# A graph and attention layer on one core: the query products bank by bank in place of four banks together, and early loads for them into the dead x area

## The reference

```python
xn = _layernorm(x)
x = x + gnn(xn, edges) + mix(xn)        # two RGAT convolutions; linear attention
x = x + ffn(_layernorm(x))              # int8 product

# mix, 12 heads of 64
q, k, v = split(xn @ W_qkv + b_qkv)
qf, kf = _phi(q), _phi(k)
kv = einsum('bhnd,bhne->bhde', kf, v)
y = einsum('bhnd,bhde->bhne', qf, kv) / max(einsum('bhnd,bhd->bhn', qf, kf.sum(2)), EPS)
mix = y @ W_out + b_out

# one RGAT convolution (4 heads, then 1)
xr = einsum('nd,rdf->rnf', x, W);  oi, oj = xr[etype, dst], xr[etype, src]
alpha = leaky_relu(oi @ q + oj @ k, 0.2)
a = softmax of alpha over the edges of each dst
out = segment_sum(a * oj, dst) + b
```

## Time and profile before

| | us |
|---|---|
| median of 3 runs (lowest, highest) | 1672.69 (1670.72, 1677.49) |
| the profiled execution | 1673.72 |
| its span | 1672.0 |
| TensorE busy | 1574.0 (94%) |
| VectorE busy | 1313.5 (79%) |
| ScalarE busy | 809.4 (48%) |
| GpSimd busy | 144.4 (9%) |
| mean granted TensorE clock | 0.978 of full |

### The profile page before, as it was taken

The page is one execution under the profiler, slowest core; times in us unless marked ns, Lnnn a source line. Parts: engine busy times, 40 slices in busy tenths (PEclk is TensorE's granted clock), DMA queues, the critical chain, the costliest instruction groups (busy, mean ns, idle before and its releaser), DMA issues.

```text
span 1672.0 us, 34410 instructions
## 1 busy us (share of the span) xinstructions
PE 1574.0 (94%) x10567; PEld 1139.5 (68%) x10568; DVE 1313.5 (79%) x2633; ACT 809.4 (48%) x1074; POOL 144.4 (9%) x280
## 2 busy tenths in 40 slices
PE   5899998988999999999999999989999999999987
PEld 4566675666556666699999999976555555555544
DVE  7699968989489999288898998972774577777795
ACT  6331115552235664378888888962222233333352
POOL 3000000000100000000000000000000143333340
PEclk9999998999999999999999999989999999999998
DMA  6111115520456663540132033023766521101212
GB/s 208 37 60 59 60 48 175 165 81 29 133 190 217 201 199 115 177 131 31 62 94 62 31 115 118 14 89 98 210 204 187 203 79 56 53 3 56 89 38 93
DMA packets 129294, 178.54 MB, mean 107 GB/s; under 512 B 15509, under 2 KB 100606, under 8 KB 129202
## 3 DMA queue, kind: packets, MB, share of 16 engines
q1 hardware_dynamic: 129202, 177.38, 33.7%
HBM read 120.47 MB, written 56.88 MB: 106 GB/s over the span
## 4 chain that ended last, share of the span: by engine, by line
PE 71%; issue 15%; DVE 7%; ACT 2%; DMA 2%; DVEq 1%; POOL 0%; SPq 0%; POOLq 0%; ACTq 0%
PE ps L2219 23%; PE ps L2173 14%; PE ps L2279 7%; PE ps L2278 7%; PE ps L1993 4%; PE ps L2084 3%; PE ps L1980 2%; PE ps L1981 2%; PE ps L1982 2%; DVE oh_q L1472 1%; PE ps L2290 1%; PE ps L2156 1%; DVE oh_p L1473 1%; PE ps L2036 1%; ACT q_m L1092 1%
## 5 line engine op out<-in xcount | busy, mean ns | idle before, releaser
L2219 PE MATMUL ps<-xrh,pf 128*128 (+1 forms) x2400 | 399.0, 329 | 4.8 <-DVE pf L1758 4.8
L2219 PEld LDWEIGHTS ps<-xrh,pf 128*128 128x128 f32 x2400 | 392.5, 190 | 11.2 <-issue 9.0
L1980 PE MATMUL ps<-w_hi,xt_hi 128*128 128x384 f16 x600 | 197.6, 329 | 10.0 <-DVE ev_t L1507 3.4
L2278 PE MATMUL ps<-x,ph 128*128 (+1 forms) x600 | 195.2, 325 | 11.8 <-POOL pl L991 11.8
L1758 DVE SCALAR_TENSOR_TENSOR pf<-vb,CT 128x1260 f32<-128x1260 f32 x118 | 172.8, 1468 | 33.6 <-PE ps L2219 33.6
L1981 PE MATMUL ps<-w_lo,xt_hi 128*128 128x384 f16 x600 | 197.4, 329 | 0.0
L1982 PE MATMUL ps<-w_hi,xt_lo 128*128 128x384 f16 x600 | 197.2, 329 | 0.0
L2279 PE MATMUL ps<-x,ph 128*128 (+1 forms) x600 | 196.5, 328 | 0.0
L1472 DVE TENSOR_SCALAR oh_q<-pat,codeT,neg_w 125x630 f16<-125x630 uint16 x420 | 185.0, 441 | 13.8 <-PE ps L1993 7.7
L1754 DVE SCALAR_TENSOR_TENSOR vb<-vb,tb 128x1260 f32<-128x1260 f32 x118 | 170.0, 1466 | 12.7 <-ACT vb L1226 11.8
L1666 DVE CUSTOM_DVE_ANT_0 tt_junk<-kbc,mb 126x1260 bf16<-126x1260 f32 x120 | 169.1, 1466 | 11.7 <-issue 11.7
(11 more groups left out here) (266 smaller groups left out, 2359.1 us busy)
## 6 DMA issues: line engine op xcount, KB each, us to landing
qbc<-tq_d SPq DMA_DIRECT2D x12, 1260.0 KB, 6.5
wst<-in_L_gnn_W SPq DMA_DIRECT2D x60, 192.0 KB, 3.2
xr_d<-ev SPq DMA_DIRECT2D x60, 192.0 KB, 2.0
x_d<-ev SPq DMA_DIRECT2D x60, 192.0 KB, 2.4
mb_d<-mb SPq DMA_DIRECT2D x30, 310.1 KB
mb<-mb_d SPq DMA_DIRECT2D x30, 310.1 KB
xrh<-xr_d SPq DMA_DIRECT2D x3, 2880.0 KB, 15.5
x<-x_d SPq DMA_DIRECT2D x2, 3840.0 KB, 18.1
```

The lines of the kernel that those rows point to most:

```text
L1980: pe.matmul(ps[:, bank, 0:CW], a_hi, hi[:, k, :], start=(k == 0), stop=False)
L2219: mm = pe.matmul(out[b], pf[j][:, b * DB:b * DB + P], x, start=(first and b % 2 == 0), stop=False, skip_group_check=True)
L2278: pe.matmul(ps[:, bank, 0:CW], p, cols(off, off + CW), start=start, stop=False, skip_group_check=True)
```

## The change

The loops of the query products are turned: bank outermost, then the six chunks, then the three split steps. Each bank's 18 matmuls follow each other, and its `q_done` is signalled when they are done. Counted in steps of three matmuls (m from 0 to 23 in a block), windows stand at 8, 16 and the end, weight tiles at every fourth. ScalarE's and VectorE's work in a block is put in an order to match: exponentials and outputs of banks 0 and 1 after the second window's one-hots, those of 2 and 3 later, one weight tile of the next block between them. Tile 0 is drawn ahead of the first block.

The loads of q, k, the three biases and weight tiles 0 to 3 move on SyncE from behind `kvs_done` to between the key windows' and the value windows' stores, into the area of x; tiles 4 and 5 stay behind `kvs_done`. Since the first weight buffer now covers `orow`, its load moves behind all windows' stores.

```diff
--- before.py
+++ after.py
@@ -166,17 +166,17 @@
-        wt = [place(f"wt{j}", [P, D], F32, (148480 if j < 3 else 76864) + 3072 * j) for j in range(6)]
+        wt = [place(f"wt{j}", [P, D], F32, (67584, 86080, 89152, 92224, 148480, 151552)[j]) for j in range(6)]
...
-        qk = place("qk", [P, K6, 2, 2 * H], F16, 158016)
-        qk2 = place("qk2", [P, K6, 2, 2], F16, 158272)
+        qk = place("qk", [P, K6, 2, 2 * H], F16, 95552)
+        qk2 = place("qk2", [P, K6, 2, 2], F16, 95744)
...
-        qkn = place("qkn", [P, K6, 2, H], F32, 157696)
-        qkn2 = place("qkn2", [P, K6, 2], F32, 157888)
+        qkn = place("qkn", [P, K6, 2, H], F32, 95296)
+        qkn2 = place("qkn2", [P, K6, 2], F32, 95488)
...
@@ -620,6 +620,26 @@
+            def wq_load(t):
+
...
+            sp.wait_ge(ln_done, NB)
+            sp.dma_start(qkn[:, :, 0, :], q1.rearrange("(k p) h -> p k h", p=P), allow_slow_non_contiguous=True).then_inc(qk_ready, 16)
...
+            for t in range(4):
+                wq_load(t)
             for c in range(2):
@@ -631,25 +651,7 @@
                 store_window(sp, W_S + k, cb, k % 2)
 
             sp.wait_ge(kvs_done, 2)
-            sp.dma_start(qkn[:, :, 0, :], q1.rearrange("(k p) h -> p k h", p=P), allow_slow_non_contiguous=True).then_inc(qk_ready, 16)
...
-            for t in range(6):
+            for t in range(4, 6):
                 wq_load(t)
             sp.wait_ge(ob_step, 6)
             sp.dma_start(ob_d.rearrange("j (p c) -> p j c", c=K6), osplit[:, :, :]).then_inc(ob_io, 16)
@@ -658,15 +660,15 @@
                     for t in ((0, 1), (2, 3), (4,), (5,))[u] if QW == 4 else ((0, 1), (2, 3), (4, 5))[u]:
                         wq_load(6 * q + t + 6)
                     store_window(sp, W_Q + QW * q + u, cc_, (QW * q + u) % 2)
-                if q == 0:
-                    sp.wait_ge(ob_io, 16)
-                    sp.dma_start(orow[:, :], ob_d[:, :]).then_inc(ob_io, 16)
                 if q == 1:
                     chunk_load(7)
             for i in range(NB):
                 for w in block_windows(i):
                     store_window(sp, w, cc_, (w - W_Q) % 2)
 
+            sp.wait_ge(wt_lo_done, WT_TILES)
+            sp.wait_ge(ob_io, 16)
+            sp.dma_start(orow[:, :], ob_d[:, :]).then_inc(ob_io, 16)
             sp.wait_ge(y_lo, 2 * NB)
             sp.wait_ge(wt_used, WT_TILES)
             sp.wait_ge(ct_out[0], 16 * 31 + 16)
@@ -1075,23 +1077,35 @@
                     act.wait_ge(wt_used, t - 2)
                 act.activation(wt_hi[t % 3][:, :], wt[t % 6][:, :], ACT.Copy, scale=SPLIT).then_inc(wt_hi_done, 1)
 
+            def exponential(q, g):
+
+                n = q * NRG + g
+                act.wait_ge(q_done, n + 1)
+                if n >= NRG:
+                    act.wait_ge(q_out, n - NRG + 1)
+                act.activation(q_m[g][:, :], ps[:, g, 0:RG], ACT.Relu, bias=nbq[:, q:q + 1], scale=-1.0).then_inc(q_mm, 1)
+                act.wait_ge(q_mm, n + 1)
+                act.activation(q_m[g][:, :], q_m[g][:, :], ACT.Exp, scale=-1.0).then_inc(q_ee, 1)
+
             act.wait_ge(bq_done, 1)
+            wt_high(0)
             for c in range(2):
                 for fb in range(3):
                     q = 3 * c + fb
                     wa = W_Q + QW * q
-                    for k in range(K6):
-                        if k in (2, 4, 5)[:QW - 1]:
-                            late_out(wa + (2, 4, 5).index(k))
-                        wt_high(6 * q + k)
-                    for g in range(NRG):
-                        n = q * NRG + g
-                        act.wait_ge(q_done, n + 1)
-                        if n >= NRG:
-                            act.wait_ge(q_out, n - NRG + 1)
-                        act.activation(q_m[g][:, :], ps[:, g, 0:RG], ACT.Relu, bias=nbq[:, q:q + 1], scale=-1.0).then_inc(q_mm, 1)
-                        act.wait_ge(q_mm, n + 1)
-                        act.activation(q_m[g][:, :], q_m[g][:, :], ACT.Exp, scale=-1.0).then_inc(q_ee, 1)
+                    wt_high(6 * q + 1)
+                    late_out(wa)
+                    wt_high(6 * q + 2)
+                    wt_high(6 * q + 3)
+                    exponential(q, 0)
+                    exponential(q, 1)
+                    wt_high(6 * q + 4)
+                    late_out(wa + 1)
+                    wt_high(6 * q + 5)
+                    exponential(q, 2)
+                    if q + 1 < K6:
+                        wt_high(6 * q + 6)
+                    exponential(q, 3)
                     late_out(wa + QW - 1)
                 w_hi_part(C_O + c)
 
@@ -1571,28 +1585,41 @@
                 dve.wait_ge(wt_hi_done, t + 1)
                 dve.scalar_tensor_tensor(wt_lo[k % 3][:, :], wt[k][:, :], SPLIT, wt_hi[k % 3][:, :], ALU.mult, ALU.subtract).then_inc(wt_lo_done, 1)
 
-            def query_block(q):
+            def query_out(q, g):
+
+                n = q * NRG + g
+                dve.wait_ge(q_ee, n + 1)
+                dve.scalar_tensor_tensor(sub(QF, q)[:, g * RG:(g + 1) * RG], ps[:, g, 0:RG], sub(bq1, q), q_m[g][:, :],
+                                         ALU.add, ALU.max).then_inc(q_out, 1)
+
+            def query_block(q, more=True):
 
                 wa = W_Q + QW * q
-                for k in range(K6):
-                    wt_low(6 * q + k, k)
-                    if k in (1, 3, 4)[:QW - 1]:
-                        count_part(wa + (1, 3, 4).index(k) + 1)
-                for g in range(NRG):
-                    n = q * NRG + g
-                    dve.wait_ge(q_ee, n + 1)
-                    dve.scalar_tensor_tensor(sub(QF, q)[:, g * RG:(g + 1) * RG], ps[:, g, 0:RG], sub(bq1, q), q_m[g][:, :],
-                                             ALU.add, ALU.max).then_inc(q_out, 1)
+                wt_low(6 * q + 1, 1)
+                count_part(wa + 1)
+                wt_low(6 * q + 2, 2)
+                wt_low(6 * q + 3, 3)
+                query_out(q, 0)
+                query_out(q, 1)
+                count_part(wa + 2)
+                wt_low(6 * q + 4, 4)
+                wt_low(6 * q + 5, 5)
+                query_out(q, 2)
+                if more:
+                    wt_low(6 * q + 6, 0)
+                query_out(q, 3)
                 count_part(wa + QW)
 
+            wt_low(0, 0)
             count_part(W_Q)
             dve.wait_ge(ct_out[0], 16 * (3 * NB // 2 + 2) + 16)
             dve.wait_ge(ct_out[1], 16 * (3 * NB // 2 + 1) + 16)
             dve.wait_ge(bq_done, 1)
             query_block(0)
             w_lo_part(5)
-            with dve.Fori(1, K6) as q:
+            with dve.Fori(1, K6 - 1) as q:
                 query_block(q)
+            query_block(K6 - 1, False)
 
             def normalised(i):
 
@@ -2065,26 +2092,27 @@
                 for fb in range(3):
                     wa = W_Q + QW * (3 * c + fb)
                     of_w = [window(pe, wa + u)[1:] for u in range(QW)]
-                    for k in range(K6):
-                        if k in (2, 4, 5)[:QW - 1]:
-                            u = (2, 4, 5).index(k)
-                            count_window(wa + u, 6, *of_w[u])
-                        t = 6 * (3 * c + fb) + k - 2
-                        if t == 0:
-                            pe.wait_ge(kvd_done, 2)
-                            pe.wait_ge(qk_ready, 70)
-                        if t >= 0:
-                            wq_tile(t)
-                        w_h, w_l = w_hi[cc % 2][:, k, fb * P:(fb + 1) * P], w_lo[cc % 2][:, k, fb * P:(fb + 1) * P]
-                        for step, (w, t) in enumerate(((w_h, xt_hi), (w_h, xt_lo), (w_l, xt_hi))):
-                            for g in range(NRG):
-                                n = (3 * c + fb) * NRG + g
-                                if k == 0 and step == 0 and n >= NRG:
-                                    pe.wait_ge(q_out, n - NRG + 1)
-                                last = pe.matmul(ps[:, g, 0:RG], w, t[:, k, g * RG:(g + 1) * RG], start=(k == 0 and step == 0),
-                                                 stop=(k == K6 - 1 and step == 2))
-                                if k == K6 - 1 and step == 2:
-                                    last.then_inc(q_done, 1)
+                    for g in range(NRG):
+                        n = (3 * c + fb) * NRG + g
+                        for k in range(K6):
+                            m = 6 * g + k
+                            if m % 4 == 0:
+                                if m in (8, 16):
+                                    count_window(wa + m // 8 - 1, 6, *of_w[m // 8 - 1])
+                                t = 6 * (3 * c + fb) + m // 4 - 2
+                                if t == 0:
+                                    pe.wait_ge(kvd_done, 2)
+                                    pe.wait_ge(qk_ready, 70)
+                                if t >= 0:
+                                    wq_tile(t)
+                            if k == 0 and n >= NRG:
```

(7 more changed lines are left out.)

25 lines of the change are left out of this document (12 added, 13 removed).

## The result

| | before | after |
|---|---|---|
| median, 5 runs each | 1673.35 (1670.72 to 1677.49) | 1661.52 (1656.61 to 1665.3) |
| profiled execution, span | 1673.72, 1672.0 | 1656.61, 1654.9 |

The ratio is 0.992, 95% interval 0.9893 to 0.9947. In a second series the changed kernel had 1659.48 against 1673.47, ratio 0.9911 (0.9895 to 0.9927).

A forecast was written before the change was run, and what follows sets the result against it. VectorE was taken to bound the query stage, its 11.72 us of idle time being the possible gain. 11.7 - 0.5 (clock) - 0.2 (odd waits) = 11.0 us off a 1672.69 median gave 1661.7 us, range 1658.5 to 1668.5.

The forecast's parts named there:

- VectorE bounds the query stage before: Query stage: VectorE busy 115.77 of 127.49 us, so the change can give its idle time, 11.72 us.
- The block, 18.23: Settled query block: 18.23 us instead of 19.09, with no wait of VectorE left.
- the sum: Whole kernel: 11.7 less 0.5 for the clock and 0.2 for odd waits, 11.0 us gained.
- the walk: Query block stepped through three engines with trace durations: each output finds its exponential ready 1.4 to 3.7 us ahead.
- The early loads, 3.8: Start of the query stage: the 3.8 us wait of the first weight tile's low part goes entirely.
- The issue gap, zero: Ahead of one-hots after outputs: the held window-word read's gap goes at both places; upper end 0.49 us each.
- The clock, 0.5: Start of the query stage: one shorter TensorE stretch at 1.2 GHz, taken to cost 0.5 us.
- One bank back to back, nil: Query products: successive products adding into one bank cost nothing, as already in the values stage.
- rival 3: Query products into one bank do not overlap their weight load: 40 us more on TensorE, about 1695 us; chance 0.04.
- The values stage, nil: Values stage: GpSimd's moved small instructions cost nil by the rows, the delayed window store nil, at most 3 us.
- Rival 1: Query blocks: outputs still wait for late exponentials, blocks of 19.2 us, gain only 5 to 7 us, 1667; chance 0.17.
- The whole, 1661.7: Whole kernel: forecast median of 1661.7 us, against 1672.69 before; chance 0.64.

The follow-up runs named there:

- thin low parts: Kernel before, VectorE's low part of each weight tile cut from 768 columns to 8: settled block 19.08 us, median 1670.82 us, ratio 0.9977.
- the earlier read: Kernel before, window word of the block's last window read ahead of the four outputs: settled block 19.09 us, median 1671.94 us, ratio 0.999.
- TensorE's turn: Kernel before with only TensorE's product loops turned bank by bank, loads and other engines' order as before: median 1663.91 us, ratio 0.9948.
- ScalarE late: Changed kernel, exponentials of banks 0 and 1 moved behind two high parts and a window copy in ScalarE's queue: block 24.0 us, 1695.37 us, one run.
- early loads alone: Kernel before with only the loads moved (q, k, biases, weight tiles 0 to 3 earlier, orow later): median 1670.62 us, ratio 0.9979.

## Why the prediction held, point by point

- *VectorE bounds the query stage before: wrong.* Its idle time was read as what bounds, but the settled block was the ring of 14.6 + 3.9 + 0.6 us; thin low parts and the earlier read left it at 19.1. The step that failed is the first one, "what the change can give is VectorE's idle time": taking it out at the read, or taking 4.4 us of work a block off VectorE, gave a settled block nothing. The block came out well all the same, because breaking the ring gives the time down to the next bound, and that is VectorE's busy time, the figure that I had subtracted; TensorE's 17.4 lie only 0.5 below it. This part was luck. The earlier trace rows had a sign of it: three outputs in 1.60 us, 0.53 each, where after the change two take 1.00 and start 0.46 apart. They were not slower: an output waited there too, for less than the list of waits tells, since ScalarE ends an exponential only every 0.92 us (the pairs that start at 320.16 and 322.93 above are the first and the fourth).
- *The block, 18.23: 0.33 too long.* Four outputs at 0.53 were mis-sized, 4 x 0.07 = 0.28; the measured block is 3 x 3.61 + 6 x 0.87 + 4 x 0.46 = 17.9. Over six blocks that is 2.0 of the 2.8 us that the sum lacked (11.0 against 13.79). No output waits, as the walk had it, but the walk's margins of 1.4 to 3.7 us are counted to the ends of the outputs; to their starts it gives 0.8 to 3.2, and in the block from 291.27 they were 1.3 to 3.0.
- *The early loads, 3.8: right as to the wait.* It went entirely. The loads are worth more than it, in the query stage 5.52 alone and 5.00 on top of TensorE's turn (123.04 - 118.04). VectorE started the low part of tile 0 at 243.90 with no wait. But the order that I walked, with this low part ahead of the one-hots, depends on the loads: without them it waits 6.58 us.
- *The issue gap, zero: right.* It goes when the outputs' waits go, it goes when the word is read earlier, and it comes back as the outputs wait (ScalarE late). By the Trainium skill's rule (Advanced Engine Details and Errata, Sequencer Loop), as the prediction takes it, the read would not have been held back; the trace of before and these runs speak against that.
- *The clock, 0.5: nothing.* TensorE waited 1.53 + 0.24 + 0.84 = 2.61 us for the first one-hots where I had 3.2, and the granted clock stayed at 1.00 from 241.0 to 262.0. That is the next 0.5 of the difference.

```profile
246.04 0.70 PE L2020 MATMUL ps<-oh_q,oh_p 125*128 125x315 f16 x4 [1.53 <-DVE oh_p L1487]
246.98 0.72 PE L2020 MATMUL ps<-oh_q,oh_p 125*128 125x315 f16 x4 [0.24 <-DVE oh_p L1487]
248.53 0.99 PE L2020 MATMUL ps<-oh_q,oh_p 125*128 125x315 f16 x6 [0.84 <-DVE oh_p L1487]
```

- *One bank back to back, nil: right.* Bank 0's first products start 0.136 us apart (eighteen distances from 241.08 to 243.53), so rival 3 did not come.
- *The values stage, nil: right.* `kvd` starts at 239.47 for 239.44, and the copy at the earlier trace rows's 141.55 starts at 141.64. In other runs `kvd` starts up to 1.1 us later, but that offset stands already at the window copy near 107 us (107.19 before, 108.30 with the early loads alone), ahead of the first moved load at about 123, so it isn't theirs. The bias row costs nothing: TensorE's wait ahead of its product is for VectorE.
- *Rival 1* did not come in the change; ScalarE late shows it real, with its place in ScalarE's queue, when the exponential comes 4.07 us after VectorE wants it. Its price is then far above what I gave it (1695 in one run, for 1667), since a late output also stops TensorE.
- *The whole, 1661.7 for 1661.52: luck in the last microseconds.* The sum lacked 2.8 us in the two stages, and the medians differ by 11.8 where the stages differ by 13.8.

## What to carry to other kernels

An engine with little idle time need not be the bound: follow one buffer round all engines (product, exponential, output, next product) and add up, and if that gives the block's length, shortening any work outside of the ring brings nothing there. Break such a ring by making its pieces end at different times, then look for the next bound, and move that engine's work into stretches where it waits anyway. Idle engines are not free helpers where they share something with the busy one.

## What the hardware showed that I had not expected

In the operations seen here GpSimd and VectorE held each other up until the other's instruction was over, in both directions. In the changed kernel GpSimd's small preparation runs beside VectorE's subtraction of the weights:

```profile
133.41 0.44 POOL L950 CAST bsplit<-bres 128x6 bf16<-128x6 f32 x1
133.93 2.56 POOL L952 TENSOR_TENSOR bcol<-bres,bsplit 128x6 f32<-128x6 f32 x1
136.55 0.19 POOL L954 CAST bsplit<-bcol 128x6 bf16<-128x6 f32 x1
```

```profile
133.89 2.54 DVE L1512 TENSOR_TENSOR w_lo<-wst,w_hi 128x2304 f16<-128x2304 f32 x1
136.36 0.54 DVE L1564 TENSOR_TENSOR V<-ps,bk_bc 128x384 f32 x1
```

Six columns took 2.56 us, as long as VectorE's operation of 2.54; where GpSimd made them apart from it, they took 0.20. VectorE's large one-hots beside the 0.2 us instructions kept their 0.43 to 0.45 us, and one small one took 0.35 for 0.24. So the price was nil in the earlier trace rows and 4.3 us a piece with a long instruction: it is set by how much of the other engine's instruction is left. Not every pair is held: VectorE's addition from PSUM at 129.53 (`V<-ps`, 0.56 us) ran over GpSimd's subtraction at 129.76, which kept its 0.27 us (0.28 before).
